# The last layer's depthwise convolution, from its preparation stage to GpSimd in the attention loop

## The reference

```python
q = x @ wq.T + bq
k = (x @ wk.T + bk) * scaling
v = x @ wv.T + bv
lepe = jax.lax.conv_general_dilated(v, lepe_w, window_strides=(1, 1), padding=[(2, 2), (2, 2)],
        dimension_numbers=('NHWC', 'HWIO', 'NHWC'), feature_group_count=C) + lepe_b
qr, kr = theta_shift(qh, sin, cos), theta_shift(kh, sin, cos)
attn = jax.nn.softmax(jnp.einsum('bnld,bnmd->bnlm', qr, kr) + mask, axis=-1)
out = jnp.einsum('bnlm,bnmd->bnld', attn, vr)
out = jnp.swapaxes(out, 1, 2).reshape(B, H, W, -1) + lepe
return out @ wo.T + bo
```

## Time and profile before

| | us |
|---|---|
| three executions | 8042.01, 8057.19, 8063.88 |
| median | 8057.19 |
| span of the profiled execution | 8043.7 |

### The profile page before, as it was taken

The page is one execution under the profiler, slowest core; times in us unless marked ns, Lnnn a source line. Parts: engine busy times, 40 slices in busy tenths (PEclk is TensorE's granted clock), DMA queues, the critical chain, the costliest instruction groups (busy, mean ns, idle before and its releaser), DMA issues. The chain is left out here.

```text
span 8043.7 us, 157230 instructions
## 1 busy us (share of the span) xinstructions
PE 7011.3 (87%) x56704; PEld 4290.7 (53%) x56704; DVE 4978.2 (62%) x7151; ACT 3803.5 (47%) x7049; POOL 2019.4 (25%) x2407
## 2 busy tenths in 40 slices
PE   3999999999877899469999999997776799999999
PEld 2555555555555556345555555553332466666665
DVE  4555555555555666445555555554888577777776
ACT  0444444444522555224444444443111577777777
POOL 3344344334220000043443443441111000000000
PEclk7999999999988989779999999998766899999999
DMA  7776776776459756477667667664222555455453
GB/s 160 154 140 122 139 136 117 138 140 122 88 178 216 133 110 122 103 163 141 124 129 142 126 124 140 133 123 96 77 72 72 138 124 136 121 130 130 120 135 88
DMA packets 500587, 1025.92 MB, mean 128 GB/s; under 512 B 80391, under 2 KB 276680, under 8 KB 460568
## 3 DMA queue, kind: packets, MB, share of 16 engines
q1 hardware_dynamic: 452694, 932.07, 53.5%
q0 software_dynamic: 47360, 86.53, 6.6%
HBM read 670.94 MB, written 358.93 MB: 128 GB/s over the span
## 5 line engine op out<-in xcount | busy, mean ns | idle before, releaser
L1512 DVE TENSOR_REDUCE a_nmp<-a_S 128x2 f32<-128x1024 f32 x1536 | 1878.8, 1224 | 1153.3 <-PE a_S L1357 1139.9
L1616 ACT ACTIVATE a_PROB<-a_T 128x512 f32<-128x512 f32 x3072 | 1667.7, 595 | 1750.0 <-PE a_T L1336 1742.5
L1215 POOL CAST a_RF<-a_RL 32x512 fp32r<-32x512 f32 x1536 | 1297.7, 845 | 1138.5 <-DVE a_RL L1540 1046.6
L2397 DVE CUSTOM_DVE_ANT_0 a_X<-a_S,a_mask 128x1024 f32<-128x1024 f32 x768 | 916.9, 1222 | 466.0 <-PE a_S L2293 462.3
L2440 ACT ACTIVATE a_PROB<-a_T 128x512 f32<-128x512 f32 x1536 | 836.3, 602 | 291.6 <-PE a_T L2307 291.6
L1332 PE MATMUL a_T<-a_QW,a_KW 64*128 64x512 f32 x3072 | 799.5, 513 | 181.1 <-ACT a_PROB L1616 108.2
L1332 PEld LDWEIGHTS a_T<-a_QW,a_KW 64*128 64x128 f32 x3072 | 309.5, 190 | 1161.0 <-issue 1157.9
L1370 PE MATMUL a_O<-a_PROB,a_V 128*32 128x512 f32 x6144 | 898.8, 660 | 2.5 <-ACT a_PROB L1616 2.5
L2307 PE MATMUL a_T<-a_ident,a_X 128*128 128x128 f32 x6144 | 827.4, 278 | 3.7
L2307 PEld LDWEIGHTS a_T<-a_ident,a_X 128*128 128x128 f32 x6144 | 671.2, 141 | 201.3 <-issue 183.1
L1357 PEld LDWEIGHTS a_S<-a_KV,a_QV 64*128 64x128 f32 x6144 | 650.2, 199 | 120.8
(11 more groups left out here) (178 smaller groups left out, 9248.2 us busy)
## 6 DMA issues: line engine op xcount, KB each, us to landing
a_QV<-a_part_rows SPq DMA_DIRECT2D x384, 256.0 KB, 7.7
a_rel_rows<-a_RF SPq DMA_DIRECT2D x96, 1024.0 KB, 9.2
a_K<-part_rows SPq DMA_DIRECT2D x576, 128.0 KB, 4.1
a_part_rows<-a_part SPq DMA_DIRECT2D x48, 1024.0 KB, 16.9
a_QV<-a_part_rows SPq DMA_DIRECT2D x384, 128.0 KB, 8.2
a_QV<-a_rel_rows SPq DMA_DIRECT2D x384, 128.0 KB, 7.9
a_QW<-a_rel_rows SPq DMA_DIRECT2D x192, 256.0 KB, 9.9
a_mask<-L_mask SPq DMA_DIRECT2D x48, 1024.0 KB, 8.6
```

Source lines behind the costliest of these rows:

```text
L1215: nc.gpsimd.tensor_copy(dst, src).then_inc(permuted, 1)
L1512: nc.vector.tensor_reduce(nmp[:, qh, c, 2 * pr:2 * pr + 2, kh], S[:, pr], AX.X, ALU.max).then_inc(s_done, 1)
L1616: nc.scalar.activation(PROB[:, s % PRING, 2 * pr + sd], T[:, slot(("st", s, pr, sd))], ACT.Exp).then_inc(t_act, 1)
L2397: nc.vector.tensor_tensor_reduce(out=X[:, v % 2, c, g], in0=S[:, sd].rearrange("p a b -> p (a b)"), in1=mask[:, n % 2, g, c], scale=1.0, s ...
```

## The change

The preparation no longer convolves, projects or stores a result. ACT copies the layer's input with bo added to XB (`begin`), and SP stores it as the start of the output; this takes the place of the DRAM-to-DRAM copies. The padded values VP are stored to DRAM (six DMAs a pair of images), in the order in which the loop wants them: by head group, with the two images of a pair on alternate 16-partition blocks. The bias of the token values comes from a 97th row of XN, set to one. Odd images' values and wo take the other 16 of 32 partitions of each head, so that the outputs of a unit lie where the convolution's do; pick follows.

In the loop, POOL computes the convolution for two units at a time (a pair of images, one quarter, one group of heads): 25 multiplies (the first also adds the bias) and 24 adds, each over 128 partitions and 8x32 pixels, half of them ahead of each of two stores. SP loads the 12 padded rows for it (`surroundings`). DVE's `divide` gets a second instruction, which adds the convolution to the divided outputs, and waits for POOL's taps. Projection and store then carry both. Apart from this, the second layer's and this layer's stores of the values go one at a time, each waiting for the one before, and so do the accumulating stores of the second layer's attention.

The core of the diff:

```diff
@@ prepare_win, attend_win (second layer)
                 sp.wait_ge(t_dve, done(b, ("v", 5, 0), "dve"))
+                need(sp, v_stored, 16 * b)
                 alone(sp)
-                sp.dma_start(v_rows[b], VT[:, b % 2]).then_inc(v_stored[b % 2], 16)
+                sp.dma_start(v_rows[b], VT[:, b % 2]).then_inc(v_stored, 16)
...
-                pool.dma_start(stream[u % IMAGES], Y[:, u % 2], accum_op=ALU.add).then_inc(y_stored[u % 2], 16)
+                need(pool, y_stored, 16 * u)
+                alone(pool)
+                pool.dma_start(stream[u % IMAGES], Y[:, u % 2], accum_op=ALU.add).then_inc(y_stored, 16)
@@ prepare_rot, sync
-            for b in range(IMAGES):
-                sp.dma_start(stream_out[b], x_in[b]).then_inc(consts_loaded, 16)
             for b in range(IMAGES):
+                p, odd = divmod(b, 2)
                 if b + 2 < IMAGES:
                     x_is_loaded(sp, b)
                     sp.wait_ge(xn_ready, 2 * b + 2)
+                    sp.wait_ge(begun, 2 * b + 2)
                     alone(sp)
                     sp.dma_start(X[:, b % 2], x_in[b + 2]).then_inc(x_loaded[b % 2], 16)
+                sp.wait_ge(begun, 2 * b + 2)
+                need(sp, x_stored, 16 * b)
+                alone(sp)
+                sp.dma_start(stream_out[b], XB[:, b % 2]).then_inc(x_stored, 16)
+                if odd:
+                    sp.wait_ge(t_act, TALLY[("vc", p, 2, 1)])
+                    need(sp, vp_stored, VP_STORES * p)
+                    alone(sp)
+                    for i in range(2 * GROUPS):
+                        j, upper = divmod(i, 2)
+                        image, hg = divmod(i, GROUPS)
+                        sp.dma_start(vp_rows[p, hg].rearrange("(g o d) y x -> o g d (y x)", o=2, d=DIM)[image],
+                                     VP[64 * upper:64 * upper + 64, p % 2, j].rearrange("c y x -> c (y x)")
+                                     ).then_inc(vp_stored, 16)
@@ prepare_rot, tensor: values (projected and outputs are gone)
-                    for k in range(2):
-                        nc.tensor.matmul(T[:, slot(n), here], XN[:, b % 2, k, P * c:P * c + P], wv[:, k],
-                                         start=k == 0, stop=False)
-                    last = nc.tensor.matmul(T[:, slot(n), here], one_line[:], bv_line[:], start=False, stop=True)
+                    for k, rows in enumerate((slice(0, HALF + 1), slice(0, HALF))):
+                        last = nc.tensor.matmul(T[:, slot(n), here], XN[rows, b % 2, k, P * c:P * c + P], wv[rows, k],
+                                                start=k == 0, stop=k == 1)
@@ prepare_rot, vector: tap is gone, and
-                    if b:
-                        for q in range(len(mine) * i // PIECES, len(mine) * (i + 1) // PIECES):
-                            tap(p, *mine[q])
...
-            for j, k in TAPS_EVEN:
-                tap(IMAGES // 2 - 1, j, k)
@@ prepare_rot, scalar: outputs is gone, and ahead of each image's padded values
+            def begin(b):
+
+                x_is_loaded(act, b)
+                need(act, x_stored, 16 * (b - 1))
+                alone(act)
                 for m in range(2):
+                    nc.scalar.activation(XB[:, b % 2, m], X[:, b % 2, m], ACT.Identity, bias=bo[:, m:m + 1]).then_inc(begun, 1)
@@ attend_rot, sync
+            def surroundings(d):
+
+                n, p = divmod(d, IMAGES // 2)
+                hg, qq = divmod(n, 4)
+                need(sp, taps, TAP_STEPS * (d - 1))
+                need(sp, vp_loaded, 16 * d)
+                alone(sp)
+                sp.dma_start(VP[:, d % 2].rearrange("c y x -> c (y x)"),
+                             vp_rows[p, hg, :, ROWS_Q * qq:ROWS_Q * qq + ROWS_Q + TAPS - 1].rearrange("c y x -> c (y x)")
+                             ).then_inc(vp_loaded, 16)
...
                 values(v - 1)
+                if v % 2 and v // 2 + 1 < DUOS:
+                    surroundings(v // 2 + 1)
@@ attend_rot, gpsimd
-            for v in range(UNITS):
-                store(v)
+            def multiply(d, k):
+
+                hg = d // (IMAGES // 2) // 4
+                dy, dx = divmod(k, TAPS)
+                src = VP[:, d % 2, dy:dy + ROWS_Q, dx:dx + SIDE]
+                if k == 0:
+                    pool.wait_ge(vp_loaded, 16 * (d + 1))
+                    if d >= 2:
+                        pool.wait_ge(t_dve, upto(2 * d - 2, "turn", "dve"))
+                    alone(pool)
+                    nc.gpsimd.tensor_scalar(CV[:, d % 2].rearrange("p (y x) -> p y x", x=SIDE), src, lw[:, hg, 0:1],
+                                            lb[:, hg:hg + 1], ALU.mult, ALU.add).then_inc(taps, 1)
+                else:
+                    need(pool, taps, TAP_STEPS * d + (added(k - 3) if k > 3 else 0))
+                    alone(pool)
+                    nc.gpsimd.tensor_scalar(PR[:, k % 3].rearrange("p (y x) -> p y x", x=SIDE), src, lw[:, hg, k:k + 1],
+                                            None, ALU.mult).then_inc(taps, 1)
+
+            def add(d, k):
+
+                pool.wait_ge(taps, TAP_STEPS * d + (added(k - 1) if k > 1 else 2))
+                alone(pool)
+                nc.gpsimd.tensor_tensor(CV[:, d % 2], CV[:, d % 2], PR[:, k % 3], ALU.add).then_inc(taps, 1)
+
+            def some_taps(d, first, last):
+                for k in range(first, last):
+                    multiply(d, k)
+                    if k > 1:
+                        add(d, k - 1)
+                if last == N_TAPS:
+                    add(d, N_TAPS - 1)
+
+            pool.wait_ge(consts_loaded, CONSTS)
+            for d in range(DUOS + 1):
+                for half in range(2):
+                    if d < DUOS:
+                        some_taps(d, *((0, N_TAPS // 2), (N_TAPS // 2, N_TAPS))[half])
+                    if 0 <= 2 * d - 2 + half < UNITS:
+                        store(2 * d - 2 + half)
@@ attend_rot, vector: divide
-                nc.vector.tensor_tensor(OSB[:], OSB[:], T[:, slot("turn"), 0:2 * P], ALU.mult).then_inc(t_dve, 1)
+                nc.vector.tensor_tensor(OSB[:], OSB[:], T[:, slot("turn"), 0:2 * P], ALU.mult).then_inc(tail_dve, 1)
+                eng.wait_ge(taps, TAP_STEPS * (v // 2 + 1))
+                eng.wait_ge(tail_dve, 2 * v + 2)
+                alone(eng)
+                nc.vector.tensor_tensor(OSB[:], OSB[:], CV[:, v // 2 % 2], ALU.add).then_inc(t_dve, 1)
```

More of the change, by code:

```diff
@@ L247, in prepare_win @@
         k_stored = [sem(f"k{m}_stored") for m in range(2)]
-        v_stored = [sem(f"v{s}_stored") for s in range(2)]
+        v_stored = sem("v_stored")
         const = ((wq, "wq_all"), (wk, "wk_all"), (wv, "wv_all"), (bq, "bq_all"), (bk, "bk_all"), (bv, "bv_all"),
@@ L593, in attend_win @@
         widened = sem("widened")
-        y_stored = [sem(f"y{s}_stored") for s in range(2)]
+        y_stored = sem("y_stored")
         out_of = {"act": t_act, "dve": t_dve}
@@ L1700, in slot @@
         return AT[n] % RING
[L1703 to L1708, removed]
     with ExitStack() as ctx:
@@ L1854, in _ @@
                         root(b + 1)
-                if b % 2 and b > 1:
-                    store(b - 3)
-                    store(b - 2)
-            store(IMAGES - 2)
-            store(IMAGES - 1)
-            pool.wait_ge(y_stored, 16 * IMAGES)
         @block.tensor
@@ L1884, in padded @@
                     for k in range(2):
-                        last = nc.tensor.matmul(T[at:at + count, slot(n)], wv[:, k, first:first + count],
-                                                XN[:, odd, k, t * BANK:(t + 1) * BANK], start=k == 0, stop=k == 1)
+                        last = nc.tensor.matmul(T[at:at + count, slot(n)], wv[0:HALF, k, first:first + count],
+                                                XN[0:HALF, odd, k, t * BANK:(t + 1) * BANK], start=k == 0, stop=k == 1)
                 last.then_inc(t_ready, 1)
@@ L1894, in rotated @@
                     last = nc.tensor.matmul(T[:, slot(n)], (wqk if what == "qk" else wqkr)[:, g, k],
-                                            XN[:, b % 2, k, h * BANK:(h + 1) * BANK], start=k == 0, stop=k == 1)
+                                            XN[0:HALF, b % 2, k, h * BANK:(h + 1) * BANK], start=k == 0, stop=k == 1)
                 last.then_inc(t_ready, 1)
@@ L1945, in _ @@
                     values(b, j)
-                if odd and p:
-                    outputs(p - 1)
-            outputs(IMAGES // 2 - 1)
         @block.vector
@@ L2072, in padded @@
                 if t == 0:
-                    need(act, taps, PAIR_TAPS * (p - 1))
+                    need(act, vp_stored, VP_STORES * (p - 1))
                 alone(act)
@@ L2107, in _, with attend_rot, added @@
                     values(b, j)
-                if odd and p:
-                    outputs(b - 3)
-                    outputs(b - 2)
-            outputs(IMAGES - 2)
-            outputs(IMAGES - 1)
```

(8 more changed lines are left out.)

145 lines of the change are left out of this document (54 added, 91 removed).

## The result

The changed kernel takes 8168.55 us (median of 4 runs, 8164.03 to 8173.41); beside it on the same chip the kernel before took 8053.95 (4 runs, 8042.01 to 8063.88). The ratio is 1.0147, interval 1.013 to 1.0165: slower by 1.5%, where 7765 us had been forecast. The profiled execution has a span of 8164.7 us, 121 more than before.

What follows compares the result with a forecast made beforehand. VectorE was taken to bound the preparation and TensorE the loop, with GpSimd just inside. 8043.7 - 323 + 29 + 2 = 7752 us of span, plus 13.5 to the median: 7765 us; range 7690 to 7960.

Steps and rivals of the forecast that it cites:

- Preparation: Stage before the attention loop: without the convolution TensorE sets the pace, 39.5 us an image, next stage near 5927; 323 us saved.
- D: Rival, chance 0.09: the preparation keeps an unseen stall, such as part stores behind the new ones, and saves 240; 7850 us.
- The additions: GpSimd's 24 two-input adds of 128x256 per pair of units in the loop, priced at 0.74 us each.
- Stores: GpSimd's store issues in the loop, 0.96 us each, two per pair of units.
- The multiply: GpSimd's 25 scalar multiplies of 128x256 per pair in the loop, without a profile row; between 0.40 and 0.74, taken as 0.46 us.
- holds: VectorE and GpSimd delaying each other in the loop: half of VectorE's 7.4 us a pair, bringing 31.2 to 35 of 36.2.
- Rival B: Chance 0.07: in the loop a multiply costs 0.74 us and everything is serialised, 45.6 us a pair; 8187 us.
- turning point: Loop cost at which slower or faster is decided: 21.4 us a unit, 0.63 us a multiply if all is serialised.
- VectorE let in after one instruction: In the loop, a held VectorE instruction gets in after one GpSimd instruction, as a cast did after 0.76 us.
- C: Rival, chance 0.04: VectorE gets in only after a whole run of GpSimd taps in the loop, 23.2 us a unit; 8226.
- VectorE's addition on the chain: In the loop, between two row maxima, the new addition costs TensorE 0.3 us a unit, 29 us in all.

Runs made afterwards that it cites:

- no_taps: The changed kernel without the convolution's 25 multiplies and 24 additions, its result a tile of zeros, VectorE's addition kept; 7738.75 us, ratio 0.9626.
- two_imm: The changed kernel with a second operation, add of an immediate 0.0, in each of a pair's 24 multiplies; 8664.0 us, ratio 1.0734.
- two_ops: The changed kernel with a second operation, add of a zero read through a pointer, in each of a pair's 24 multiplies; 7967.63 us, ratio 0.9915.
- serial_imm: As two_imm, but each GpSimd instruction waits for the one before it to end; 7977.18 us, ratio 0.9904.
- gated_imm: As two_imm, but with eight waits a pair: before every third tap GpSimd waits for one more VectorE scaling; 7767.76 us, ratio 0.9634.
- gated_one: The changed kernel, multiplies of one operation, with eight waits a pair of GpSimd on VectorE's scalings; 8176.99 us, ratio 1.0164.

## Why the prediction was wrong

- **Preparation: right.** Forecast 323 us saved, next stage at 5927; measured 313, at 5937.68. Of the ten missing, five arose before the stage, whose first load went from 5577.36 to 5582.51 though I had said that its start doesn't move; within the stage 318 are saved. D did not happen. no_taps shows the gain in the time: 301 us (8039.59 - 7738.75).
- **The additions: right.** 0.74 us forecast by halving a 128x512 instruction, 0.71 measured. Stores: 0.96 taken, 0.66 measured.
- **The multiply: the step that failed.** "I take 0.46, nearer to the copy, as it reads one tensor." It takes 0.89. It lies outside both of my bounds, 0.40 and 0.74, which assumed that a one-input instruction can't cost more than a two-input one. The pair came to 45.1 us instead of 35.0, and the multiplies are that difference: 24 x 0.89 + 0.53 = 21.9 against 11.5, +10.4; additions and stores -1.3; holds 4.9 against 3.8. A rule of the Trainium skill that I weighed there ("GPSIMD Engine Reference", Engine selection: one-input work at about line rate) had pointed the same way, and the trace contradicts it for this form.
- **Rival B** had 0.07 and was right in size: 45.6 us a pair, 8187 us, against 45.1 and 8168.55. Its make-up was not: a dearer multiply (0.89 for 0.74), fewer holds (4.9 us for 7.4). Its turning point, 0.63 us a multiply, was passed.
- **VectorE let in after one instruction: wrong too, and hidden by the first error.** I gave C 0.04, as a VectorE cast got in after 0.76 us inside a run of casts. Had the multiply cost about what I took, 7765 would not have come either: two_imm, at 0.44, takes 8664, and two_ops, at 0.52, 7968. C's mechanism is right for an unbroken row of quick instructions (two_imm, and two_ops at times), and not for the changed kernel's own row, whose longest scaling is 2.52 us. Its size was too small: it let two thirds of VectorE's work come behind the run (23.2 us a unit), where two_imm's stores come 27.9 us apart. The row that spoke for it, the normalise of 12.88 us across three memsets, was the nearer one. The Trainium skill's rule ("SBUF — State Buffer", Who interferes with whom: whole instruction, whoever issues first) agrees with the traces for gaps of 0.17 us between instructions (serial_imm, longest scaling 1.33 us). The way I read it, that VectorE is let in after one instruction, fails for quick rows without gaps (12.3 us in two_imm, 13.2 in two_ops).
- **VectorE's addition on the chain:** 29 us forecast; no_taps, where nothing of GpSimd's holds it, came to 18.12 us a unit as before. Too high.
- The forecast's figure, 7765, is met by gated_imm (7768), which is 289 us faster than the kernel before beside it and 401 than the changed one. It is 29 us above no_taps, but 17 of these lie between the two chips; by the ratios (0.9634 and 0.9626) the two can't be told apart.

Still open: why the form with one operation is the slow one (only that it is, beside three others in one kernel, is shown), why VectorE gets in beside it, and why two_ops is shut out only at times where two_imm is in nearly each unit; a difference in how exactly the instructions follow each other was not tried by itself.

## What to carry to other kernels

Price an instruction in the very form that it will have, operations and operands counted, and run one before a loop is moved onto it: a second, idle operation (add 0.0) halved this one. Then look at the other engine's longest instruction, not only at the time: an engine that has time to spare can still stop another, and a shorter instruction can make that worse (two_imm). When GpSimd works beside VectorE, break its runs at points where VectorE is due, with a wait on VectorE's own semaphore. This pays only where GpSimd's row fits: in gated_one, where it doesn't, the same waits gave nothing.

## What the hardware showed that was not expected

- GpSimd, 128x256 f32 in SBUF: scalar multiply by a pointer, no second operation, 0.89 us; with add of a pointer 0.52; with add 0.0 or times 1.0 0.44; two-tensor addition 0.71.
- An unbroken run of quick GpSimd instructions (0.44 or 0.52 us and 0.71 in turn) kept one VectorE scaling waiting for up to 13.2 us. Gaps of 0.17 us were enough to let it in, and mostly a multiply of the slow form was, too.
- Only some of VectorE's instructions are held: in two_imm the row maxima, which read PSUM, never exceeded 1.226 us, while the in-place scaling beside them, which reads and writes SBUF, went to 12.3. That the maxima fell into GpSimd's pauses doesn't explain it: in the changed kernel, where GpSimd has hardly any, none of the 768 takes over 1.226 us. The rows of two_imm:

```profile
L2406 DVE CUSTOM_DVE_ANT_0 a_X<-a_S,a_mask x768: 1205/1220/1226, 5969.9 to 8644.3; 128x1024 f32<-128x1024 f32 x192
L2413 DVE TENSOR_SCALAR a_X<-a_X,a_rmax x384: 740/750/12329, 5972.2 to 8645.5; 128x1024 f32<-128x1024 f32 x192
```
